# The expert part of a macaron block in float32: four column groups per pair, biases on transposed values, three pairs of up matrices in SBUF

## What is computed

```python
x = x + 0.5 * ffn(_layernorm(x))
x = x + attention(_layernorm(x))
x = x + 0.5 * ffn(_layernorm(x))
```

```python
o = q + _mha(q, x, x, ...)                       # 16 slots per sequence
h = _layernorm(os, e_ln_g, e_ln_b)
u = silu(einsum('besd,edf->besf', h, e_W1) + e_b1)
g = silu(einsum('besd,edf->besf', h, e_Wg) + e_bg)
y = einsum('besf,efd->besd', u * g, e_W2) + e_b2
o = o + y.reshape(Bx, NS, D)
out = _mha(x, o, o, ...)
```

## Time and profile before

| | us |
|---|---|
| median of three runs | 2881.3 |
| the three runs | 2869.48, 2881.3, 2883.99 |
| the profiled execution, its own time | 2868.0 |
| its span | 2866.2 |
| first dispatch, SP's first load to the end | 22.6 to 183.4 |
| first expert part | 183.5 to 340.6 |
| second expert part | 2532.6 to 2682.6 |
| all matrices that one expert part loads itself (pairs 2 to 7) | 37.75 MB |

### The profile page before, as it was taken

One profiled execution on the slowest core, in us unless ns is written; L12 is line 12 of the kernel. 1 busy time (PEld: TensorE's weight loads), 2 busy tenths in 40 slices (PEclk: granted clock), 3 DMA queues, 4 the chain that ended last, 5 costly groups with the idle time before them and its releaser, 6 DMA issues. The chain is left out here.

```text
span 2866.2 us, 53184 instructions
## 1 busy us (share of the span) xinstructions
PE 2625.8 (92%) x17304; PEld 1943.7 (68%) x17304; DVE 1793.2 (63%) x3172; ACT 1645.7 (57%) x4057; POOL 1429.9 (50%) x1257
## 2 busy tenths in 40 slices
PE   5988799489999999999999999999999987987899
PEld 4753377367777777777777777777777765743476
DVE  4742177466667767667767666677677666732376
ACT  2322144277777777677777776777777762322243
POOL 1100144276676776666767766767767641100242
PEclk9999899799999999999999999999999998999999
DMA  6349644322232222222322222322222216449543
GB/s 207 123 166 360 235 144 139 109 55 48 52 62 45 53 60 47 53 48 54 64 45 53 60 47 52 63 46 54 56 52 53 46 30 213 164 174 374 188 150 113
DMA packets 157472, 298.00 MB, mean 104 GB/s; under 512 B 30352, under 2 KB 108816, under 8 KB 153104
## 3 DMA queue, kind: packets, MB, share of 16 engines
q1 hardware_dynamic: 157200, 294.65, 37.6%
HBM read 185.50 MB, written 41.94 MB: 79 GB/s over the span
## 5 line engine op out<-in xcount | busy, mean ns | idle before, releaser
L1313 ACT ACTIVATE att_prob<-att_ps_s,att_nmax 128x512 f32<-128x512 f32 (+3 forms) x1024 | 529.3, 528 | 287.8 <-DVE att_nmax L1209 287.3
L1120 POOL TENSOR_TENSOR att_z_sb<-att_z_sb,att_cos 128x512 f32<-128x512 f32 x256 | 330.6, 1291 | 419.6 <-DMA att_zs<-att_z_sb 419.6
L1470 PE MATMUL att_ps_p<-sh_ident,att_prob 128*128 128x128 f32 x2560 | 395.8, 277 | 26.4 <-DVE att_probT L1221 18.7
L1209 DVE TENSOR_REDUCE att_nmax<-att_ps_s 128x2 f32<-128x1024 f32 (+3 forms) x512 | 410.2, 822 | 13.3
L1232 DVE TENSOR_TENSOR att_oT_lo<-att_on,att_oT_hi 128x512 fp32r<-128x512 f32 x128 | 137.8, 1077 | 410.2 <-ACT att_oT_hi L1343 410.2
L1123 POOL TENSOR_TENSOR att_z_sb<-att_z_sb,att_zs 128x512 f32<-128x512 f32 x256 | 338.2, 1321 | 20.1
L1470 PEld LDWEIGHTS att_ps_p<-sh_ident,att_prob 128*128 128x128 f32 x2560 | 288.5, 140 | 79.2 <-DVE att_probT L1221 34.6
L1121 POOL TENSOR_TENSOR att_zs<-att_zs,att_sin 128x512 f32<-128x512 f32 x256 | 330.5, 1291 | 0.0
L1481 PE MATMUL att_ps_p<-att_probT,att_v_sb 128*64 128x512 f32 (+3 forms) x2048 | 306.2, 441 | 4.2 <-ACT att_probT L1338 2.4
L1481 PEld LDWEIGHTS att_ps_p<-att_probT,att_v_sb 128*64 128x64 f32 x2048 | 138.7, 137 | 175.8 <-issue 135.1
L1338 ACT COPY att_probT<-att_ps_p 128x512 f32<-128x512 f32 x384 | 215.9, 600 | 57.9 <-PE att_ps_p L1470 57.2
(11 more groups left out here) (177 smaller groups left out, 5901.2 us busy)
## 6 DMA issues: line engine op xcount, KB each, us to landing
ffn_w<-in_e_W SPq DMA_DIRECT2D x64, 1024.0 KB, 17.3
att_zs<-att_z_sb SPq DMA_DIRECT2D x1024, 64.0 KB, 2.3
ffn_wg<-in_e_Wg SPq DMA_DIRECT2D x32, 1024.0 KB, 15.5
x_normalised_transposed<-dis_b_xnT SPq DMA_DIRECT2D x32, 512.0 KB, 2.9
com_b_xnT<-x_normalised_transposed SPq DMA_DIRECT2D x32, 512.0 KB, 4.4
dis_b_x<-in_x SPq DMA_DIRECT2D x16, 512.0 KB, 3.7
com_b_x<-in_x SPq DMA_DIRECT2D x16, 512.0 KB, 3.9
x_after_ffn<-com_b_xo SPq DMA_DIRECT2D x32, 256.0 KB, 2.4
```

What stands on the lines that cost most here:

```text
L1120: nc.gpsimd.tensor_tensor(z[:, m, i, :], z[:, m, i, :], cos[:], ALU.mult)
L1209: nc.vector.tensor_reduce(nmax[:, p % 2, qt, :], ps[:, :, at:at + (qt + 1) * P], AX.X, ALU.max, negate=True)\
L1313: nc.scalar.activation(prob[:, p % 2, hh, PLACE[qt]], ps[:, hh, at:at + (qt + 1) * P], ACT.Exp, bias=nmax[:, p % 2, qt, hh:hh + 1], accum_ ...
L1470: last = nc.tensor.transpose(turn_bank(p, k)[:, at:at + P], prob[:, p % 2, hh, PLACE[qt]][:, kb * P:(kb + 1) * P], g.ident[:])
```

## The change

It rewrites `expert_phase`, and with it `expert_loads`, `ExpertRing` and SP's part of the dispatch.

- `up` of a pair is one set of 16 products on four column groups (W1 and Wg of both experts), in two halves of 512 columns. Its PSUM tile is one of two. The stage copy of L515 is gone: PE reads the padded rows `hP`.
- The tile is copied to SBUF without bias, the first half by ACT and the second by DVE (`evict`), and transposed by PE as eight 128x128 pieces (`turn`). DVE adds the biases to the transposed values, of 16 rows instead of 32 per group (`biased`), ACT takes one silu over 512 elements, DVE multiplies u and g (`gate`).
- `down` has four column groups too: two for the experts, two for the halves of the sum over 1024. `add_halves` multiplies y by a 0/1 matrix `sel`, which transposes and adds the halves.
- The biases come once, as `bT1` of 128 x 8 x 4 x 8, in four DMAs with pieces of 32 bytes. These and the nine tables are loaded at the start of the dispatch.
- W1 and Wg have a third place, `more`, in SBUF that the dispatch's tiles leave free; it exists in the expert phase alone. Most small tiles of the phase lie in `at_all`.
- W1 and Wg of pair 2 are loaded without a wait; later pairs wait until `up` of the pair three before is done.
- The value product's first half goes to ACT and its second to DVE.
- Keys and values of the first seven pairs are made before `down(7)`. All loops of the phase are written out.
- SP waits at the end of the dispatch until the last stores have landed.

```diff
-        self.b1, self.bg = sb("b1", [2 * QUAD, 2, F]), sb("bg", [2 * QUAD, 2, F])
+    UP, DOWN, TABS = 3, 2, 9 + 4
+        self.bT1 = sb("bT1", [P, NE // 2, 4, FK])
...
+            for dst, src in expert_tables(io, ring):
+                sp.dma_start(dst, src).then_inc(ring.tab_in, 16)
             bodies(sp, B // NB, body)
+            for at in xt_out:
+                sp.wait_ge(at, 16 * B // 2)
...
+        more = [sb(x, [P, 2, DC, F]) for x in ("w1", "wg")]
+        w_up = [[ring.w1[:, i], ring.wg[:, i]] for i in range(DOWN)] + [[w[:] for w in more]]
...
+            def load_up(pr):
+                if pr >= UP:
+                    sp.wait_ge(up_mm, 2 * (pr - UP + 1))
+                for w, src in zip(w_up[pr % UP], (io["e_W1"], io["e_Wg"])):
+                    for e in range(2):
+                        sp.dma_start(w[:, e], src[2 * pr + e].rearrange("(c p) f -> p c f", p=P)).then_inc(ring.up_in[pr % UP], 16)
+            def load_down(pr):
+                sp.wait_ge(y_mm, pr - DOWN + 1)
+                ...
+            load_up(2)
+            load_up(3)
+            load_up(4)
+            for pr in range(2, NP - 3):
+                load_down(pr)
+                load_up(pr + 3)
+            for pr in range(NP - 3, NP):
+                load_down(pr)
...
+            def up(pr):
+                if pr == 0:
+                    pe.wait_ge(hb_s, DC)
+                pe.wait_ge(ring.up_in[pr % UP], 64 * (pr // UP + 1))
+                ...
+                for half in range(2):
+                    for ch in range(DC):
+                        for m in range(2):
+                            for e in range(2):
+                                last = nc.tensor.matmul(ps_up[pr % 2][(2 * m + e) * QUAD:(2 * m + e + 1) * QUAD, half * 512:(half + 1) * 512],
+                                                        hP[:, ch, 2 * pr + e, :], w_up[pr % UP][m][:, e, ch, half * 512:(half + 1) * 512],
+                                                        start=(ch == 0), stop=(ch == DC - 1))
+                    last.then_inc(up_mm, 1)
+            for pr in range(NP):
+                up(pr)
+                turn(pr)
+                if pr >= 1:
+                    down(pr - 1)
+                    add_halves(pr - 1)
+            keys_values(0, NP - 1)
+            down(NP - 1)
+            add_halves(NP - 1)
+            keys_values(NP - 1, NP)
...
+            for pr in range(NP):
+                evict(pr)
+                biased(pr)
+                gate(pr)
+                if pr >= 1:
+                    finish(pr - 1)
```

More of the change, by code:

```diff
@@ L232, in experts @@
             def experts(pair, i):
[L233 removed]
+                for dst, src, at in expert_loads(io, ring, pair)[2 * i:2 * i + 2]:
                     sp.dma_start(dst, src).then_inc(at, 16)
@@ L437, in expert_phase @@
[L437 to L445, removed]
@@ L517, in step @@
-            def step(pr, par, h, first=False, second=False, last=False):
-                if not last:
-                    hidden(pr + 1, 1 - par, first)
-                for i, (bias, ps, pre) in enumerate(((b1, ps_u, ub), (bg, ps_g, gb))):
-                    dve.wait_ge(up_mm.sem, up_mm.at(pr, i + 1))
-                    if not first and i == 0:
-                        dve.wait_ge(ugT_mm.sem, ugT_mm.at(pr, 0))
-                    nc.vector.tensor_tensor(pre[:], ps[0:R, :], bias[:, par, :], ALU.add).then_inc(pre_s.sem, 1)
-                dve.wait_ge(silu_s.sem, silu_s.at(pr, 2))
-                nc.vector.tensor_tensor(ub[:], ub[:], gb[:], ALU.mult).then_inc(ug_s.sem, 1)
-                if not first:
-                    finish(pr - 1)
@@ L612, in _ @@
[L612 to L628 removed]
+                last.then_inc(done, 1)
@@ new lines, in add_halves @@
+            def add_halves(pr):
+                pe.wait_ge(y_s, pr + 1)
+                if pr >= 1:
+                    pe.wait_ge(on_s, pr)
+                else:
+                    pe.wait_ge(sel_s, 1)
+                for ch in range(DC):
+                    last = nc.tensor.matmul(ps_yT[:, ch * 2 * B:(ch + 1) * 2 * B], y[:, ch * P:(ch + 1) * P],
+                                            sel[:].rearrange("p e b -> p (e b)"), start=True, stop=True)
+                last.then_inc(yT_mm, 1)
@@ L662, in _, with evict @@
-            copy_hidden(NP - 1)
+            for t in range(2):
+                nc.scalar.activation(attnT[:, t, :], ps_v[:, t, :], ACT.Identity, bias=g.bv_pad[:, t:t + 1]).then_inc(va_s, 1)
+            def evict(pr):
+                act.wait_ge(up_mm, 2 * pr + 1)
+                if pr >= 2:
+                    act.wait_ge(turn_mm, pr - 1)
+                nc.scalar.copy(pre[pr % 2][:, 0:512], ps_up[pr % 2][:, 0:512]).then_inc(prea_s, 1)
+            def silu(pr):
+                act.wait_ge(bias_s, pr + 1)
+                nc.scalar.activation(act_in[:], act_in[:], ACT.Silu).then_inc(silu_s, 1)
```

333 lines of the change are left out of this document (158 added, 175 removed).

## The result

The changed kernel takes 2807.4 us (median of 4 runs, 2803.6 to 2809.6) against 2881.5 before (4 runs, 2869.5 to 2884.0): ratio 0.975, 95% interval 0.972 to 0.978, so 74 us or 2.5% faster. The prediction was 2833 us with a range of 2810 to 2858: the sign was right, and the gain was larger than the range allowed. The profiled execution took 2808.4 us, its span 2806.6.

What follows compares the result with a forecast made beforehand. Weight loads were taken to bound the expert parts, between front and tail. Savings of 25.7 and 20.2 us, less 0.5 per dispatch, gave 2868.0 - 45 = 2823; 10.3 for run spread made it 2833, range 2810 to 2858.

Steps and rivals of the forecast that it cites:

- What bounds the parts: Expert parts: a front of 25 us with little loaded, a DMA-set stream of 113.5 and 109.5 us, and a tail.
- Front: Start of each expert part: split value product and fewer waits start up(0) 2.2 us earlier; the stream starts 2.4 us earlier.
- Third place: Pair 2's W1 and Wg, 4.19 MB, load in the empty start of each part: 11.7 and 11.3 us gained.
- Up product on four groups costs nothing more: Expert up product: W1 and Wg together take 3.6 us at the high clock, where two products took 7.2.
- Rival D: Up and down products: four groups streaming different matrices do not run together, PE sets the part, 3030 us; chance 0.04.
- Dispatch: 13 more DMAs on SP before x of unit 2: nearly hidden, bounds 0 and 4 us, 0.5 taken in each part.
- Tail: Part's end, after W2 of pair 5 lands: one chain of 25 us plus 2 for the clock.
- rival B: More gained: high clock at the parts' ends, first stream at 372 GB/s, faster up(0); 60 us saved, 2818; chance 0.06.
- the waits of SP are met: Stream: SP's loads never wait long; only W2 of pair 7 is tight, with 5.9 us of pair 6's W2 under way.
- 33.55 MB at 358 and 372 GB/s: New stream at the old mean rates: from 205.9 and 2556.5 to 299.6 and 2646.7, against 322 and 2668.5.
- the whole stream is explained by bytes: Old stream: 40.9 MB in 113.5 us is 360 GB/s, in 109.5 us 373, so its bytes set its length.
- Rival C: No gain: the stream is slower than thought, at 280 GB/s nothing is left, 2878 us; chance 0.05.

Runs made afterwards that it cites:

- the rows with the wait: Changed kernel with a semaphore wait between the products of W1 and those of Wg in each up product: 2811.3 us, ratio 0.976.
- the version with the loops changed: Changed kernel with the up product's loops reordered so that the program has all products of W1 ahead of those of Wg: 2803.1 us, ratio 0.975.

## Why the prediction was right in sign and too small

Right, by its own steps:

- *What bounds the parts* (front, stream by bytes, tail): the runs fit it. Bytes put back over 128 partitions cost their time at the stream's rate, and an up product longer by 2.3 us in the stream costs nothing.
- *Front*: up(0) was to run from 198.6 to 204.5; it ran from 198.25 to 203.94. SP's first load of the stream went out 20.8 us after the first part's start, forecast 21.2, and 21.1 us after the second's, forecast 22.7.
- *Third place*: shown by its undoing, 10.6 and 10.8 us of stream.
- *Up product on four groups costs nothing more*: shown by the rows with the wait. 1.9 us for two groups and for four. The estimate by the Trainium skill ("TensorE: Matmul & The Clock Gate", Part 3), a quarter more for each four-group set, does not hold here. Rival D is out.
- *Dispatch*: 160.4 and 160.7 us, before 160.9 and 161.0. The 13 tables went out by 31.7, x of unit 2 at 31.84. The four pieced loads landed 0.2 to 0.6 us after one another, and x of unit 2 landed at 35.9, 1.1 us later than before and 6 ahead of its use. The 0.5 us each did not appear, nor did the loss of 30 us that pieces ten times as dear would have brought.
- *Tail*: 25.6 us in the first part, 22.9 in the second, against 27. In the first, down(5) ran at the low level as forecast (3.64); in the second it took 3.22, and the products behind it ran at the high one. This is half of rival B.

Missed, but small: "the waits of SP are met". The 5.9 us of W2 of pair 6 were counted from the landing of W2 of pair 5; down(5) takes 4 of them, so by the prediction's own numbers 1.9 us are left when W2 of pair 7 goes out. In the run it was 1.2 us (down(5) ends at 282.6, W2 of pair 6 landed at 283.8), less than the 4.7 us that the first of these loads took from issue to landing. The first load of W2 of pair 7 landed 3.6 us after the load before it in both parts, where its neighbours are 2.5 apart: a gap of 1 us in each. The share of 0.82 from 276 to 290 has this gap in it and also the beginning of the fall at the end. The third place for W2 takes the gap away.

Wrong, and the cause of the miss: the step "33.55 MB at 358 and 372 GB/s". The prediction took the old stream's mean rate for the rate of the new one. 40.9 MB in 113.5 us is what had to be explained, and "the whole stream is explained by bytes" divided one by the other and could not fail. The biases were then priced as bytes, 8.8 and 8.5 us; the runs give their shape another 29 us over the two parts, and the landings show a share of it at the matrices beside them. At the higher rate W2 of pair 5 landed 95.7 us after the first part's start in place of 104.4, and 96.0 in place of 102.8 in the second: 8.7 and 6.8 us. With 1.4 and 4.1 from the tails that is 21 us, the whole difference between 131.4 and 129.8 us forecast and 121.3 and 118.9 measured.

The 8.7 and 6.8 us are themselves a sum: 29.36 MB, the stream up to that landing, at 412 GB/s and not at 358 and 372 are 10.8 and 7.7 us, the fronts gave 0.4 and 1.6, and some 2.5 us in each part went the other way. Of these, 1.1 is the time from SP's first load to the first data (2.3 us by the landings, 1.2 forecast), and 1.4 a single late landing (3.98 us after the one before it), whose cause is open.

Rival C even had the sign at hand, "only that the rate differs between the two parts, with the same pieces and no cause in view", and took it for a reason against the gain. The sentence behind it, "against it, that both are steady", is what the stretches of 4 us refute: 289 to 410 GB/s.

One thing, which is luck and no part of the forecast, made the error smaller than 21 us in the profiled execution (2823 forecast, 2808.4 measured): attention was 6.2 us longer. One made it larger for the median: 10.3 us were added since the profiled run of before was among its fastest. The profiled run of the changed kernel is not, it lies 1 us over its median. Attention, whose code no run changes, took 1845.7 to 1856.2 us over the traces of this case; whether that is all of the difference within the runs of before stays open, as only one of them has a trace.

## What to carry to other kernels

Before a mean rate is used for a stream with other contents, cut the old stream into stretches shorter than one of its steps: if the rate differs between them, something in the stream lowers it, and the upper rate is nearer to what a stream without that will have (here 410 against a mean of 358). A DMA engine share of 1.0 says that the engines are occupied, not that they move what they can (353 and 410 GB/s at 1.03 and 1.02). Loads over 64 partitions are worth taking out of such a stream or spreading over 128. And an order in the program is not a wait: to make PE do one thing after another in an experiment takes a semaphore, and the trace has to show that it did.

## What was not expected of the hardware

- A load of 262 KB over 64 partitions, between loads of matrices over 128, cost 1.2 us (kernel before) to 1.5 us (changed kernel) beyond the 0.64 us of its bytes; over 128 partitions nothing beyond its bytes. The spread over 128 partitions also halved its pieces, from 4 KB to 2 KB. The pieces of the matrices W1 and Wg are 4 KB too, so a piece of that size alone does not explain it, but no run changed only one of the two. The Trainium skill ("SBUF — State Buffer", Door 1: The DMA port swizzle) offers a mechanism: a transfer's bandwidth goes by how many of the 16 ports of SBUF its partitions reach, and partitions 0 to 63 reach eight. The runs agree with it in direction. An estimate by that rule, half the rate for the 0.26 MB, gives 0.64 us more for each load, and 1.2 to 1.5 were measured; so the rule alone does not give the size. Whether the matrices queue behind the crowded ports, or the loads are spread unevenly over the DMA engines, or something else adds to it, is not shown. No run put the biases on a set of 64 partitions that reaches all ports, which would test it; this is open.
- The full rate of the loads on this one core was 403 to 422 GB/s, by stretches of 10 us with the queue full, in all kernels without such loads.
- PE started Wg's products on idle column groups 0.03 us behind the first of W1, ahead of six instructions that stood before them in the program (in the version with the loops changed). The Trainium skill ("TensorE: Matmul & The Clock Gate", Part 3, The mechanism) has matmuls start strictly in program order; the records of this run do not agree.
- More work for PE in the stream went with a granted clock of 0.90 in place of 0.80 there, and with products at their high-clock time behind it (down(5) of the first part 1.94 us for 3.64): of 9.3 us added on the path, 2.2 showed in the lengths of the two parts.
